# Output projection of a fused gated-convolution and MLP layer: groups of four token tiles in alternating PSUM banks instead of groups of eight

## What is computed

```python
xn = _layernorm(x)
# branch 1, H = 1024, I = 2048
p = xn @ in_proj_w.T;  h, gate = p[..., :I], silu(p[..., I:])
h = (grouped causal conv over 4 tokens of h + conv_b) * gate
residual = h
hn = _layernorm(h, ln_g, ln_b)
m = silu(hn @ fc_w.T + fc_b) @ cproj_w.T + cproj_b
attn = (m + residual) @ out_w.T          # (tokens, 2048) x (2048, 1024)
# branch 2, hidden width 4096, ternary weights with a scale per output row
f = silu(tlin(xn, w1)) * tlin(xn, w2)
f = gelu(tlin(f, h1)); f = gelu(tlin(f, h2))
ffn = tlin(f, w3)
return x + attn + ffn
```

## Time and profile before

| | us |
|---|---|
| median of 3 runs | 3830.16 |
| lowest, highest | 3829.58, 4160.11 |
| the profiled execution | 3831.61 |
| span of its slowest core (core 1) | 3830.1 |
| spans of all cores | 3806.7 to 3830.1 |

### The profile page before, as it was taken

One profiled execution on the slowest core, in us unless ns is written; L12 is line 12 of the kernel. 1 busy time (PEld: TensorE's weight loads), 2 busy tenths in 40 slices (PEclk: granted clock), 3 DMA queues, 4 the chain that ended last, 5 costly groups with the idle time before them and its releaser, 6 DMA issues.

```text
span 3830.1 us, 37904 instructions; the slowest of 8 cores (3806.7 to 3830.1 us)
## 1 busy us (share of the span) xinstructions
PE 3273.5 (85%) x14744; PEld 1433.1 (37%) x14744; DVE 548.2 (14%) x996; ACT 888.7 (23%) x1007; POOL 382.4 (10%) x727
## 2 busy tenths in 40 slices
PE   2778999999999988899999999998999846656654
PEld 1333444444444433344444444443444312222221
DVE  3222000000000121100000000002233261331112
ACT  2222211111111003321111111110205772551000
POOL 0000000000000210000000000012000001001222
PEclk9889999999999999999999999999999968889977
DMA  3333444444444453344444444445322214345566
GB/s 87 66 61 57 75 77 77 77 75 75 76 76 76 70 110 66 62 75 74 77 76 75 75 77 77 77 68 88 63 39 37 33 22 66 56 71 88 89 143 159
DMA packets 112144, 284.41 MB, mean 74 GB/s; under 512 B 13281, under 2 KB 37986, under 8 KB 111970
## 3 DMA queue, kind: packets, MB, share of 16 engines
q0 software_dynamic: 100016, 256.19, 41.3%
q1 hardware_dynamic: 11954, 25.80, 2.0%
HBM read 504.54 MB, written 16.78 MB: 136 GB/s over the span
## 4 chain that ended last, share of the span: by engine, by line
PE 80%; DMA 7%; ACT 4%; issue 3%; DVE 3%; DVEq 1%; POOL 0%; ACTq 0%; POOLq 0%; SPq 0%
PE ps_mm L488 46%; PE ps_mm L419 12%; DMA ab<-cprojT 3%; PE ps_mm L656 3%; PE ps_mm L700 3%; PE ps_mm L733 3%; PE ps_mm L542 3%; PE ps_tok L542 3%; PE ps_mm L814 2%; ACT L862 2%; PE ps_mm L786 2%; PE ps_mm L998 1%; PE ps_tok L998 1%; DMA af<-x 1%; DVE ab L448 1%
## 5 line engine op out<-in xcount | busy, mean ns | idle before, releaser
L488 PE MATMUL ps_mm<-ab 128*128 128x512 bf16 x8192 | 1773.1, 379 | 7.8 <-DVE ab L448 4.2
L488 PEld LDWEIGHTS ps_mm<-ab 128*128 128x128 bf16 x8192 | 801.2, 98 | 979.6 <-issue 19.2
L419 PE MATMUL ps_mm<-ab 128*128 128x512 bf16 x2048 | 466.8, 387 | 62.8 <-DVE ab L448 61.8
L502 ACT ACT_TABLE_LOAD x128 | 164.2, 1283 | 809.8 <-PE ps_mm L488 809.8
L527 DVE TENSOR_TENSOR ab<-ab 128x512 bf16<-128x512 bf16 x128 | 54.4, 425 | 1947.1 <-DMA ab<-w3R 1901.1
L502 ACT ACTIVATE ab<-ps_mm,params_s 128x512 bf16<-128x512 f32 x256 | 175.9, 687 | 634.0 <-PE ps_mm L488 632.4
L419 PEld LDWEIGHTS ps_mm<-ab 128*128 128x128 bf16 x2048 | 199.9, 100 | 326.6 <-issue 108.1
L814 PE MATMUL ps_mm<-ab 128*128 128x512 bf16 x512 | 140.5, 428 | 96.7 <-DMA ab<-cprojT 79.0
L786 PE MATMUL ps_mm<-ab 128*128 128x512 bf16 x512 | 136.2, 432 | 74.2 <-ACT ab L796 52.7
L434 ACT ACT_TABLE_LOAD x64 | 82.1, 1283 | 499.4 <-PE ps_mm L419 499.4
L448 DVE SCALAR_TENSOR_TENSOR ab<-ps_mm,params_s,ab 128x512 bf16<-128x512 f32 x128 | 96.1, 750 | 430.1 <-PE ps_mm L419 424.1
(11 more groups left out here) (73 smaller groups left out, 1591.7 us busy)
## 6 DMA issues: line engine op xcount, KB each, us to landing
ab<-h1T POOLq DMA_DIRECT2D x128, 512.0 KB, 5.2
ab<-h2T POOLq DMA_DIRECT2D x128, 512.0 KB, 5.2
ab<-w12T POOLq DMA_DIRECT2D x64, 512.0 KB, 5.1
ab<-w3R POOLq DMA_DIRECT2D x128, 128.0 KB, 3.1
ab<-fcT POOLq DMA_DIRECT2D x32, 512.0 KB, 5.2
ab<-cprojT POOLq DMA_DIRECT2D x64, 256.0 KB, 4.3
af<-x SPq DMA_DIRECT2D x17, 512.0 KB, 3.6
scr<-af SPq DMA_DIRECT2D x32, 256.0 KB, 2.5
```

Source lines behind the costliest of these rows:

```text
L419: ins = tensor.matmul(ps_mm[bank][:, 0:NT], pan3[:, k, :], xn(k, c0 + t2 * NT, NT), start=(k == 0), stop=(k == HC - 1))
L488: ins = tensor.matmul(ps_mm[bank][:, 0:NT], pan3[:, kk, :], src_t(k, t2 * NT, NT), start=(k == 0), stop=(k == FC - 1))
L502: ins = scalar.activation(dst_t(m, t2 * NT, NT), ps_mm[bank][:, 0:NT], AF.Gelu, bias=0.0, scale=params[:, psc + m:psc + m + 1])
```

## The change

The token tiles are taken in 4 groups of 4 instead of 2 groups of 8, which makes 8 phases of 16 panels. The banks alternate by group: groups 0 and 2 use banks 0 to 3, groups 1 and 3 use banks 4 to 7; both halves of one group use the same four. The weight panels are loaded once for each group and half, so 128 panel loads take the place of 64. A panel now serves 4 matmuls instead of 8. The number of matmuls (512), of evictions, of `acc` and `xr` loads and of stores stays. The list order follows the same pattern as before with 4 tiles where there were 8. The removed `saq_wait` repeats one six lines above it. The core of the diff:

```diff
+    n_g4 = (n_tc + 3) // 4
     if trunc is None:
         _fin = []
-        for grp in range(n_grp):
+        for grp in range(n_g4):
             for half in range(2):
-                for tc in range(grp * 8, min((grp + 1) * 8, n_tc)):
+                for tc in range(grp * 4, min((grp + 1) * 4, n_tc)):
                     _fin.append((grp, half, tc))
-        for grp in range(n_grp):
+        for grp in range(n_g4):
             for half in range(2):
                 for kc in range(IC):
                     sl = kc % 4
                     wadd(f"ow_{grp}_{half}_{kc}", ring(r_owp, sl, 512),
...
-                for tc in range(grp * 8, min((grp + 1) * 8, n_tc)):
+                for tc in range(grp * 4, min((grp + 1) * 4, n_tc)):
                     ii = _fin.index((grp, half, tc))
                     wadd(f"acc_{tc}_{half}",
...
-                    ii = fin_idx[(tc2 // 8, half2, tc2)]
+                    ii = fin_idx[(tc2 // 4, half2, tc2)]
...
-    for grp in range(n_grp):
-        tcs = list(range(grp * 8, min((grp + 1) * 8, n_tc)))
+    for grp in range(n_g4):
+        tcs = list(range(grp * 4, min((grp + 1) * 4, n_tc)))
         need_nt = (tcs[-1] * 128 + 127) // NT
+        bb = (grp % 2) * 4
...
                         if kc == 0:
-                            bank_wait(tensor, j)
+                            bank_wait(tensor, bb + j)
                         ins = tensor.matmul(
-                            ps8[j], rc_t(kc, tc * 128, 128), pan,
+                            ps8[bb + j], rc_t(kc, tc * 128, 128), pan,
                             start=(kc == 0), stop=(kc == IC - 1))
...
-                    if ii >= 2:
-                        pg2, ph2, pt2 = fin_order[ii - 2]
-                        saq_wait(vector, f"ost_{pt2}_{ph2}")
                     vector.drain()
-                    vector.scalar_tensor_tensor(osts, ps8[j], 1.0, accs,
+                    vector.scalar_tensor_tensor(osts, ps8[bb + j], 1.0, accs,
                                                 ALU.mult, ALU.add)
...
-                    bank_done(j, f"ibk_{tc}_{half}")
+                    bank_done(bb + j, f"ibk_{tc}_{half}")
```

More of the change, by code:

```diff
@@ L982, in build_program, with _ @@
              kind="store", data_mark=f"ost_{tc}_{half}")
-    for grp in range(n_grp):
-        tcs = list(range(grp * 8, min((grp + 1) * 8, n_tc)))
+    for grp in range(n_g4):
+        tcs = list(range(grp * 4, min((grp + 1) * 4, n_tc)))
         need_nt = (tcs[-1] * 128 + 127) // NT
+        bb = (grp % 2) * 4
         for half in range(2):
             @block.tensor
-            def _(tensor, grp=grp, half=half, tcs=tcs, need_nt=need_nt):
+            def _(tensor, grp=grp, half=half, tcs=tcs, need_nt=need_nt, bb=bb):
                 if half == 0:
@@ L1008, in _ @@
                 @block.vector
-                def _(vector, grp=grp, half=half, j=j, tc=tc):
+                def _(vector, grp=grp, half=half, j=j, tc=tc, bb=bb):
                     ii = fin_idx[(grp, half, tc)]
```

## The result

| | before | after |
|---|---|---|
| median of 10 runs, us | 3830.6 | 3895.9 |
| ratio to the kernel before | 1 | 1.0177 (95%: 1.0149 to 1.0205) |
| span of the slowest core in the profiled execution, us | 3830.1 | 3896.4 |
| last stage, mean of the eight cores, us | 229.8 | 290.4 |

The changed kernel is slower by 1.8%: clear of no change, while the interval takes in 2%. The time lies in the forecast range of 3842 to 3902, 26 us above its likeliest value of 3870; the change is 65 us where 40 were forecast. Some executions of every kernel show one die at a lower clock throughout; they are left out, and where an experiment had few others, the last stage is compared on the cores of the undisturbed die.

What follows compares the result with a forecast made beforehand. TensorE carries the span, and only the last stage can move. Gaps and tail give back 22 us, slower phases take 61, putting the end 39.3 us above 3830.1; forecast 3870, range 3842 to 3902.

Steps and rivals of the forecast that it cites:

- loads slow at 4.8: Rival, output projection: panel loads slow under their own traffic, landing in 4.8 us, adding 29 us: 3899; slow loads' chance 0.17.
- Where the stage is bound, and that it gets slower: Last stage: gaps and tail give back 22 us, slower phases take 61, so the kernel ends 39.3 us later.
- The ring: Inside a phase: four panel slots no longer hide loads; landing 3.6 us, slot turn 5.4, twelve panels 16.2 us.
- 1 to 2 us once per turn: Sign inside a phase: TensorE's expected wait for weight panels, once per 5.4 us slot turn.
- The gap: Between phases: TensorE waits 4.9 + 5.4 + 0.2 = 10.5 us for weights, seven times instead of three.
- The first panel stands right there: In the gap: next phase's first panel is issued behind the second waiting load pair, 4.9 us after the last matmul.
- I take 5.4: In the gap: landing time of the next phase's first panel, chosen from 5.3 to 6.3 us.
- The 0.4 us for the banks: Mean wait per boundary for banks still being evicted: 0.8 us charged at the four boundaries inside a group.
- The clock: TensorE's granted clock is 0.50 only in a phase's first 4 us, costing 2.1 us per phase.
- the clock stays at 1.2 GHz: Rival: short panel waits keep TensorE at half clock through phases, 27.3 us each instead of 21.8: 3909; chance 0.08.
- The banks and the double loads: Output projection: alternating banks worth zero beyond 0.4 us; 64 more panels cost GpSimd 34 us, hidden.
- not slower: Rival: panels come as fast as used, 10.4 us instead of 16.2 per phase, 46 us less: 3824; chance 0.05.

Runs made afterwards that it cites:

- the run with everything in place: Changed kernel with eight panel slots, next phase's first eight panels before waiting loads, first two acc/xr pairs before panel 12, banks alternating every phase; ratio 0.9973, stage 227.6 us.

## Why the prediction was right, point by point

The direction, the path and the largest term were right, and the time is in the range. It also lies near the 3899 of the rival "loads slow at 4.8", but not for that reason: no median landing came near 4.8, and the 26 us above 3870 come from the gaps (15), the phases and the tail (6) and the spread of the cores (5).

*Where the stage is bound, and that it gets slower.* Right. The gaps and the tail shrink and the phases take more than that back. By the means of eight cores: gaps and tail give back 3 x 27.7 + 28.3 - 7 x 13.0 - 14.6 = 6 us (the forecast said 22), and the phases take 8 x 23.1 - 4 x 29.6 = 66 (the forecast: 61).

*The ring.* Right, and the best-sized term: phases of 23.1 us where 22.5 were forecast, a median landing of 3.9 us against 3.6, a turn of 5.3 against 5.4. The waits for panels are shorter and more frequent than the "1 to 2 us once per turn" of the prediction: six or seven in a phase, 0.6 us on the median. The rings of eight and of three confirm the form from both sides, with phases of 16.9 and 28.2 us. The rival "loads slow at 4.8" did not come. The estimate of 2.3 us from the Trainium skill ("DMA: Bandwidth & Descriptors", section "Anatomy of one DMA — SWDGE (gpsimd) path") was no guide here: medians went from 3.4 with three slots to 5.2 with eight.

*The gap.* This is the mis-sized term: 13.0 us instead of 10.9, seven times, 15 of the 21 us by which the mean stage exceeds the forecast's 269.3. Two steps of it were off, and a third term was not needed.
- "The first panel stands right there", 4.9 us after the last matmul. It came at 6.5, mainly because the first eviction started at +1.47 instead of +0.3. The f32 loads for it are issued behind the last panel, and with the ring slower than TensorE that panel is issued only 5.2 us before the phase ends (mean of 64). The prediction charged their traffic to the last panels (0.9 us), and did not charge their own lateness to the eviction. The run with the pairs moved ahead shows it: first eviction at +0.36, first panel at +5.0 in six gaps of seven. The stop of GpSimd in the seventh gap adds the rest, 2.4 us once.
- "I take 5.4" for its landing, the low end of one core's three gaps (5.30, 5.36 and 6.29), "since fewer panels follow in one burst". The mean of 24 gaps on eight cores before was 6.0 to TensorE's start, and 6.5 after. The reason doesn't hold: with 12 semaphores all four follow in one burst, and it is 6.6. It doesn't come down with half of the f32 loads either.
- The 0.4 us for the banks were not needed: the panels came after the banks were free.

*The rest.* Phases 5 us and tail 1.5 us above. The remaining 5 of the 26 us between 3870 and 3896 are the spread of the cores: the slowest core stood 11.7 us above the mean span before and 20.7 after, less 3 us by which the stage began earlier on the mean. A spread read from one execution of each is partly chance.

*The clock.* Half right. The prediction expected 0.50 only in the first 4 us of a phase, and named a fall inside phases as a sign of being wrong. It falls in each gap (0.50 in the window from 3633) and comes back some 4 us later; the window from 3640, with 0.94, still holds the last of that. But in 26 of 64 phases it falls once more, as at 3689 above. On a core that is 12 us at half clock, so at most 6 us of TensorE's work, and the waits for panels hide part of it. The 26 phases last 24.4 us on the mean and the other 38 last 22.2, but a late panel may be behind both the length and the fall. So a part of the rival "the clock stays at 1.2 GHz" came, and it can account for all of the 5 us by which the phases are above the forecast; no run separates it. The Trainium skill's "TensorE: Matmul & The Clock Gate", section "HAM oscillation — how this bites in real kernels", describes a cold start for each tile that waits for its load. The trace agrees for the gaps, and for the fall behind the wait of 2.46 us, while most waits inside a phase have no fall behind them.

*The banks and the double loads.* The alternating banks gain nothing: confirmed. GpSimd's 34 us of further issues are hidden: confirmed, since it is busy for 100 of 298 us. For the queues the prediction had a DMA share of 0.77 inside a phase, "not full"; the window from 3640 shows 0.78. That was enough as long as the ring set the pace. The doubled loads still cost about 64 us of the queues' time, and the run with everything in place, at a share of 0.92, is where that shows.

*The rival "not slower".* The ring of eight is this rival made real: stage 235.8 us, near the 229.8 of before. No panel landed within the 2.0 us that the prediction asked for (the shortest took 2.6 us, in both kernels); more slots did it instead.

## What to carry to other kernels

Halving the work that a loaded panel serves halves the time that hides the next load: compare slots x work per slot with work + issue + landing before shrinking a group, and count the queue time of the repeated loads, which no order of waits gives back. When a gap has a chain that names one releaser, look for the second bound that ends just before it, since removing the first alone may give nothing, as with the panels put ahead in the kernel before. Watch the granted clock inside the loop too: waits for loads can bring it down between two gaps. And where a stage reloads its weights for each group, ask first what space has come free by then.

## What the runs showed of the hardware

- A 128x512 panel that is read as f32 and written as bf16 (256 KB read, 128 KB written) keeps the queues for about 1.0 us (206 less 142 us for 64 of them, means of eight cores). A 256 KB f32 tile costs less: leaving out 32 of them took the stage's share times length from 206 to 182 us, about 0.8 us each.
- The landing time of the same panel depends on what is in flight: medians of 3.1 to 3.5 us on the eight cores before, 3.4 and 3.9 (means of the cores) with three and four slots that set the pace, 5.2 with eight, and 7.38 in a gap behind four f32 loads. The shortest was 2.6.
- A DMA share near 1 is reached in the gaps (1.05) and in the run with everything in place (0.92); at 0.70 on the mean the stage was not short of bandwidth but of slots, since eight slots made it 55 us shorter.
- The granted clock fell to 0.50 in the middle of 26 of 64 phases with waits for panels between the chunks, of 62 of 64 where the last four panels came late as well (a wait of 3.27 us in the row shown), and of none of 32 in the kernel before.
- GpSimd can stand still for 3.1 us at one place of its list, on all eight cores, with no releaser in the trace.
